# Attention probabilities of 51 units transposed by VectorE blocks and a DRAM exchange instead of by TensorE

## The chip, the cores and the metric

One Trainium2 chip; the kernel runs on one of its cores. The metric is the device time of one launch in microseconds (us), the median of several runs. The engines are named as in the profile: PE (TensorE, with PEld for its weight loads), DVE (VectorE), ACT (ScalarE), POOL (GpSimd) and SP (SyncE, which issues nearly all DMAs here).

## The reference, cut to what matters

A gated cross-attention layer followed by a gated feed-forward layer: B = 8 batches, S = 128 tokens, E = 512, H = 32 heads in 8 key-value groups of 4 heads, D = 128, all float32.

```
q = (layernorm(x) @ Wq) per head, k = ctx @ Wk, v = ctx @ Wv per group; q, k rotated by position
scores = q k^T / sqrt(D); masked scores = -1e9
attn = softmax(scores)                       # 128 queries x 128 keys, per batch and head
x = x + tanh(g_xattn) * (concat(attn @ v) @ Wo)
x = x + tanh(g_ffn) * FFN(layernorm(x))      # silu(x w1 + b1) * (x w2 + b2), then w3, b3
```

What the change touches is `attn @ v`: `attn` stands with queries on the partitions, and the product needs it with keys there, so each 128 x 128 block of probabilities has to be transposed.

## The kernel before

Every float32 product is made of three PE passes over hi and lo parts (`three`, L509 to L511): a value is split into a rounded hi part (ACT) and the remainder lo (DVE or POOL). The kernel has a first stage (transposes of the inputs, K and V projections, the first Q blocks, until about 115 us), then 64 **units**, and a feed-forward stage at the end.

A unit n = 16 gg + 2 c + k (`n_of`) is one key-value group (n // 8) with one batch (n % 8): 4 heads, 128 queries, 128 keys. Its steps, with the engine of each and the line in the profile:

- `scores` (PE, L632 and L633): q k^T of the four heads into `s_banks`, the one PSUM buffer for it; it waits until `mask_rest` of the unit before has read that buffer.
- `mask_first` and `mask_rest` (DVE, L1432 and L1441), then `exps` (ACT, L913, four), `recip` (DVE, L1451) and `norm` (POOL, L1185) make the probabilities in `prob[k]`.
- `prob_transpose` (PE, four transposes, L515) writes them with keys on the partitions to `t_bank`; `pT_hi_copy` (ACT) and `pT_lo_split` (DVE) make the hi and lo parts from there.
- `pv` (PE, three matmuls) into `pv_bank`, then `o_hi_copy` (ACT) and `o_lo_split` (DVE, L1306). The next `pv` waits for both, since there is one `pv_bank`.
- `out_proj` (PE, twelve matmuls) into `o_bank[k]`, and `add_out` (DVE, L1465) to the residual.

Beside each unit stands one Q block of the units to come: `q_block` (PE, twelve matmuls into `f_bank`), `cos_q` and `sin_q` (DVE, L1353), `add_q` (POOL, L1176), later `q_hi_copy` (ACT) and `q_lo_split` (POOL, L1143). One weight chunk a unit is split too (`split_chunk`, ACT and POOL); SP refills its slot of `raw` when POOL is done with it (`load_chunk`, L444).

There is no scheduler: each engine runs its own list in order, with semaphores. After a written-out first pair comes a loop of three passes over eight pairs, then (from unit 52) written-out lists in which the feed-forward weights are prepared too: `ffn_load` (SP, L483, four DMAs a tile), `ffn_tile` (DVE, L1532, a transpose of 32 x 32 blocks), `ffn_hi` (ACT), `ffn_lo` (POOL). In the loop a unit's transpose, `pv` and next unit's scores follow each other on PE like this:

```
q_block, scores(c,1), q_block, prob_transpose(c,0), out_proj(c-1,0), pv(c,0),
prob_transpose(c,1), out_proj(c-1,1), scores(c+1,0), pv(c,1)
```

## Time and profile before

| what | value |
|---|---|
| runs | 665.12 us median of 3 (665.05 to 666.77) |
| span of the profiled execution | 662.9 us (its own time is not listed apart; the median of the runs is 2.2 us above the span) |
| granted TensorE clock | 1.000 |
| PE busy | 654.6 us, 99% |
| DVE, POOL, ACT busy | 490.2 (74%), 385.5 (58%), 314.1 (47%) |
| DMA | 66.32 MB, 100 GB/s mean |

The page lists each engine's busy time and the costliest groups of instructions. A timeline row gives start, length, engine, line, operation, what is written from what, and in square brackets the idle time ahead of it with what ended it. Matmuls are pipelined, so their rows overlap: the distance of two starts tells what one costs, not its length.

### The profile page before, as it was taken

To read this page: it belongs to the slowest core of one execution; us is meant where nothing else is said; L and a number is where in the kernel's file an instruction comes from. 1 tells how busy PE (TensorE), PEld (TensorE's weight loads), DVE (VectorE), ACT (ScalarE), POOL (GpSimd) and SP (SyncE) were. 2 spreads that over 40 slices of the span, in tenths; PEclk is the share of its full clock that TensorE was granted. 3 is DMA by queue.
4 is the path that set the end of the run, shared out by engine and by line. 5 is a ranking of instruction groups with operands and counts; after the bars stand their busy time and mean duration, and the time that the engine had idled before them with its cause. 6 is when DMAs were issued, how large, how long until landed. Compare 5 with 4: busy or idle time off the path is not lost.

```text
span 662.9 us, 11265 instructions
## 1 busy us (share of the span) xinstructions
PE 654.6 (99%) x3309; PEld 550.3 (83%) x3309; DVE 490.2 (74%) x1235; ACT 314.1 (47%) x891; POOL 385.5 (58%) x323
## 2 busy tenths in 40 slices
PE   8999999999999999999999999999999999989998
PEld 7888888788888888888888888888888888878886
DVE  3987665887777777777777777777777888986432
ACT  4335613545445445544554554554455566545210
POOL 6457767875566666666556666666655776402100
PEclk9999999999999999999999999999999999999999
DMA  9996983422212131312222121212122205000002
GB/s 302 321 325 210 306 303 105 143 62 99 91 39 97 44 99 34 95 32 96 62 80 95 34 98 45 95 32 95 63 76 75 58 10 151 0 1 1 0 33 95
DMA packets 67452, 66.32 MB, mean 100 GB/s; under 512 B 6608, under 2 KB 50640, under 8 KB 67408
## 3 DMA queue, kind: packets, MB, share of 16 engines
q1 hardware_dynamic: 65984, 64.77, 30.7%
q0 software_dynamic: 384, 1.05, 0.4%
q8 instruction: 17, 0.28, 0.2%
q14 instruction: 27, 0.22, 0.1%
q10 hardware_dynamic: 1040, 0.00, 0.1%
HBM read 46.93 MB, written 18.87 MB: 99 GB/s over the span
## 4 chain that ended last, share of the span: by engine, by line
PE 94%; DVE 2%; DMA 1%; issue 1%; POOL 0%; ACT 0%; DVEq 0%
PE f_bank L509 12%; PE f_bank L511 12%; PE f_bank L510 12%; PE o_bank L509 10%; PE o_bank L511 10%; PE o_bank L510 10%; PE s_banks L632 6%; PE t_bank L515 4%; PE pv_bank L509 3%; PE pv_bank L511 3%; PE pv_bank L510 3%; PE s_banks L633 2%; PE t_bank L511 1%; PE t_bank L509 1%; PE s_banks L511 1%; PE s_banks L510 1%
## 5 line engine op out<-in xcount | busy, mean ns | idle before, releaser
L1185 POOL TENSOR_TENSOR prob<-prob,small 128x512 f32<-128x512 f32 x64 | 66.6, 1040 | 124.9 <-DVE small L1451 124.9
L913 ACT ACTIVATE prob<-prob,small 128x128 f32<-128x128 f32 x256 | 99.8, 391 | 77.7 <-DVE small L1441 72.2
L509 PE MATMUL o_bank<-wo_hi,o_hi 128*128 128x512 f32 x248 | 102.1, 412 | 0.0
L1143 POOL TENSOR_TENSOR q_lo<-q,q_hi 128x512 fp32r<-128x512 f32 x64 | 82.7, 1292 | 32.8 <-ACT q_hi L843 32.8
L509 PE MATMUL f_bank<-xT_hi,wq_hi 128*128 128x512 f32 x256 | 101.6, 397 | 0.0
L843 ACT ACTIVATE o_hi<-pv_bank 128x512 fp32r<-128x512 f32 x64 | 38.3, 599 | 131.4 <-PE pv_bank L511 130.9
L511 PE MATMUL f_bank<-xT_hi,wq_lo 128*128 128x512 f32 x256 | 99.9, 390 | 0.0
L510 PE MATMUL f_bank<-xT_lo,wq_hi 128*128 128x512 f32 x256 | 99.8, 390 | 0.0
L511 PE MATMUL o_bank<-wo_hi,o_lo 128*128 128x512 f32 x248 | 97.4, 393 | 0.0
L510 PE MATMUL o_bank<-wo_lo,o_hi 128*128 128x512 f32 x248 | 96.9, 391 | 0.0
L1353 DVE TENSOR_TENSOR t_sin<-f_bank,rope 64x512 f32<-64x512 f32 x128 | 88.1, 689 | 2.8
L1176 POOL TENSOR_TENSOR q<-t_cos,t_sin 128x512 f32<-128x512 f32 x64 | 82.7, 1293 | 4.3 <-DVE t_sin L1353 4.2
L1441 DVE CUSTOM_DVE_ANT_0 prob<-s_banks,prob 128x128 f32<-128x128 f32 x256 | 59.1, 287 | 10.3 <-DVE prob L1432 7.7
L1353 DVE TENSOR_TENSOR t_cos<-f_bank,rope 128x512 f32<-128x512 f32 x64 | 43.9, 686 | 29.5 <-PE f_bank L511 29.4
L632 PE MATMUL s_banks<-k_parts,q_hi 128*128 128x256 f32 x256 | 62.8, 323 | 0.4 <-issue 0.2
L1465 DVE SCALAR_TENSOR_TENSOR resid<-o_bank,small,resid 128x512 f32<-128x512 f32 x62 | 46.4, 748 | 17.4 <-PE o_bank L511 16.2
L633 PE MATMUL s_banks<-k_parts,q_lo 128*128 128x128 f32 x256 | 56.9, 222 | 0.0
L511 PEld LDWEIGHTS f_bank<-xT_hi,wq_lo 128*128 128x128 f32 x256 | 48.1, 188 | 10.2
L509 PEld LDWEIGHTS f_bank<-xT_hi,wq_hi 128*128 128x128 f32 x256 | 48.1, 188 | 9.5 <-issue 0.4
L510 PEld LDWEIGHTS f_bank<-xT_lo,wq_hi 128*128 128x128 f32 x256 | 48.2, 188 | 9.1
L511 PEld LDWEIGHTS o_bank<-wo_hi,o_lo 128*128 128x128 f32 x248 | 46.6, 188 | 10.6
L1306 DVE TENSOR_TENSOR o_lo<-pv_bank,o_hi 128x512 fp32r<-128x512 f32 x64 | 44.0, 687 | 15.3 <-ACT o_hi L843 15.3
(170 smaller groups left out, 1469.5 us busy)
## 6 DMA issues: line engine op xcount, KB each, us to landing
k_scratch<-ks_parts SPq DMA_DIRECT2D x16, 512.0 KB, 3.1
raw<-in_L_xattn_Wq_dram SPq DMA_DIRECT2D x32, 256.0 KB, 2.8
raw<-in_L_xattn_Wo_dram SPq DMA_DIRECT2D x32, 256.0 KB, 2.6
k_parts<-k_scratch SPq DMA_DIRECT2D x16, 512.0 KB, 3.6
v_scratch<-vs_hi SPq DMA_DIRECT2D x16, 256.0 KB, 3.9
v_scratch<-vs_lo SPq DMA_DIRECT2D x16, 256.0 KB, 4.3
v_hi<-v_scratch SPq DMA_DIRECT2D x16, 256.0 KB, 3.9
v_lo<-v_scratch SPq DMA_DIRECT2D x16, 256.0 KB, 4.3
```

The source lines that it names most:

```text
L509: nc.tensor.matmul(dst, st[0], mv_[0], start=start, stop=False)
L510: nc.tensor.matmul(dst, st[0], mv_[1], start=False, stop=False)
L511: return nc.tensor.matmul(dst, st[1], mv_[0], start=False, stop=stop)
L632: nc.tensor.matmul(s_banks[:, 256 * h:256 * (h + 1)], q_hi[:, k, h, :], k_parts[:, half, b, :], start=True, stop=False)
L633: mm = nc.tensor.matmul(s_banks[:, 256 * h:256 * h + 128], q_lo[:, k, h, :], k_parts[:, half, b, 0:128], start=False, stop=True)
L913: e = nc.scalar.activation(prob[:, k, h, :], prob[:, k, h, :], ACT.Exp, bias=nmin[k][:, h:h + 1], scale=-1.0, accum_out=psum_row[k][:, h:h ...
L1143: nc.gpsimd.tensor_tensor(dst, a, b_, ALU.subtract).then_inc(s, 1)
L1176: nc.gpsimd.tensor_tensor(q32[:, (e // 4) % 2, e % 4, :], t_cos[:, ts, :], t_sin[:, ts, :], ALU.add).then_inc(pool_rope, 1)
L1185: nc.gpsimd.tensor_tensor(prob[:, k], prob[:, k], rrow[k].unsqueeze(2).to_broadcast([128, GH, S]), ALU.mult).then_inc(pool_norm, 1)
L1353: return nc.vector.tensor_tensor(dst, a, b_, ALU.mult)
L1441: op = nc.vector.tensor_tensor_reduce(prob[:, k, h, :], s_parts[:, h, 0, :], prob[:, k, h, :], 1.0, HUGE, ALU.add, ALU.min, nmin[k][:, h:h ...
L1465: nc.vector.scalar_tensor_tensor(out=resid[:, b, :], in0=bank_of_out(gg, c, k)[:, :], scalar=tg_x, in1=resid[:, b, :], op0=ALU.mult, op1=A ...
```

## The change

For units 2 to 52 PE does no transpose. `p_blocks` on DVE transposes `prob` in 32 x 32 blocks into a new tile `p_blk`, SP stores that tile to a scratch in DRAM (`store_p`, 256 KB) and loads it back with rows and blocks exchanged (`load_p`, 256 KB in runs of 512 bytes) into `p32`. ACT makes `pT_hi` from `p32` and POOL, instead of DVE, makes `pT_lo`. Units 0, 1 and 53 to 63 keep `prob_transpose`. Since the exchange takes time, the loop is written anew: a step of unit u does the scores of u+1, the Q block, `out_proj` of u-2 and `pv` of u-1. The loop covers units 4 to 51, with written-out code ahead of it and behind it. SP's list is fully written out, with the stores and loads between the weight loads. `b3_row` gets its own place, as `p_blk` takes the old one. The diff, cut to its core:

```diff
+HEAD_T, TAIL_T = 2, 11
+        def unit(c, k, d):
+            return (2 * c + k + d) // 2, (2 * c + k + d) % 2
+        def on_pe(n):
+            return isinstance(n, int) and (n < HEAD_T or n >= 4 * UNITS - TAIL_T)
...
 # SP
+            def store_p(gg, c, k):
+                sp.wait_ge(dve_pblk, n + 1 - HEAD_T)
+                sp.dma_start(p_dram[slot * 128:(slot + 1) * 128, :], p_blk[:, k, :]).then_inc(p_stored[k], 16)
+            def load_p(gg, c, k):
+                sp.wait_ge(p_stored[k], 16 * swap_turn(gg, c))
+                if not (isinstance(n, int) and n < HEAD_T + 2):
+                    sp.wait_ge(act_pThi, n - 1)
+                    sp.wait_ge(pool_pTlo, n - 1 - HEAD_T)
+                sp.dma_start(p32[:, k, :].rearrange("p (i x) -> p i x", i=4),
+                             p_dram[slot * 128:(slot + 1) * 128, :].rearrange("(i c) (j x) -> (c j) i x", i=4, j=4)).then_inc(p_loaded[k], 16)
+            def pair(gg, c):
+                store_p(gg, c, 0); load_chunk(2 * r + 1, G + 2); load_p(gg, c, 0)
+                if r == 0 and not first: next_v(1, G)
+                store_p(gg, c, 1); load_chunk(...); load_p(gg, c, 1)
+                # then next_k(0, G + 1) at r == 1, next_v(0, G + 1) at r == 2, next_k(1, G + 1) at r == 3
...
 # PE
+            def step(gg, c, k):
+                scores(gg, *unit(c, k, 1))
+                q_block(gg, 6 + 2 * c + k)
+                out_proj(gg, *unit(c, k, -2))
+                pv(gg, *unit(c, k, -1))
...
 # ACT
             def pT_hi_copy(gg, c, k):
-                act.wait_ge(pe_pT, n + 1)
+                if on_pe(n):
+                    act.wait_ge(pe_pT, turn_of(n))
+                else:
+                    act.wait_ge(p_loaded[k], 16 * swap_turn(gg, c))
...
+                    hi(heads_by_q_block(pT_hi[:, k]), by_q_block(p32[:, k]), act_pThi)
+            def step(gg, c, k):
+                o_hi_copy(gg, *unit(c, k, -2))
+                split_chunk(*pair_chunks(gg, c)[k])
+                q_hi_copy(gg, *unit(c, k, 2))
+                exps(gg, *unit(c, k, 1))
+                pT_hi_copy(gg, c, k)
...
 # POOL
+            def pT_lo_split(gg, c, k):
+                pool.wait_ge(act_pThi, n_of(gg, c, k) + 1)
+                pool.wait_ge(pe_pv, n_of(gg, c, k) - 1)
+                nc.gpsimd.tensor_tensor(heads_by_q_block(pT_lo[:, k]), by_q_block(p32[:, k]), heads_by_q_block(f32(pT_hi[:, k])),
+                                        ALU.subtract).then_inc(pool_pTlo, 1)
+            def step(gg, c, k):
+                split_chunk(*pair_chunks(gg, c)[k])
+                q_lo_split(gg, *unit(c, k, 2))
+                norm(gg, *unit(c, k, 1))
+                add_q(gg, 6 + 2 * c + k)
+                pT_lo_split(gg, c, k)
...
 # DVE
+            def p_blocks(gg, c, k):
+                dve.wait_ge(pool_norm, n + 1)
...
+                nc.vector.transpose(p_blk[:, k, :].rearrange("p (j h b) -> p j h b", j=4, h=GH),
+                                    prob[:, k].rearrange("p h (a j) -> p j h a", j=4)).then_inc(dve_pblk, 1)
+            def step(gg, c, k):
+                mask_scores(gg, *unit(c, k, 1))
+                o_lo_split(gg, *unit(c, k, -2))
+                cos_q(gg, 6 + 2 * c + k)
+                recip(gg, *unit(c, k, 1))
+                sin_q(6 + 2 * c + k)
+                p_blocks(gg, *unit(c, k, 1))
+                add_out(gg, *unit(c, k, -2))
...
 # written-out tail: DVE, ACT and POOL ahead of exps(3, 2, 1) and norm(3, 2, 1), unit 53
             ffn_tile(0)
+            o_lo_split(3, 1, 0)
             o_lo_split(3, 1, 1)
...
             exps(3, 2, 1)
             pT_hi_copy(3, 2, 0)
...
             q_lo_split(3, 3, 0)
-            norm(3, 2, 0)
+            pT_lo_split(3, 2, 0)
             split_chunk(*pair_chunks(3, 2)[0])
             norm(3, 2, 1)
```

Three places show how the order moves. First PE ahead of the loop, in the written-out start. Before, behind the scores of unit 2 (`s_banks`, L632) comes the pv of unit 1, and the loop follows at once:

```order
L633 MATMUL s_banks<-k_parts_64,q_lo_63 128x128
L509 MATMUL pv_bank<-pT_hi_71,v_hi_65 128x512 [waits act_ohi,dve_olo,dve_pTlo,act_pThi]
L510 MATMUL pv_bank<-pT_lo_72,v_hi_65 128x512
L511 MATMUL pv_bank<-pT_hi_71,v_lo_66 128x512
L708 UNCONDITIONAL_BRANCH
```

With the change the scores of unit 3 (the row that waits for `dve_mask`) stand directly behind those of unit 2:

```order
L727 MATMUL s_banks<-k_parts_64,q_lo_63 128x128
L726 MATMUL s_banks<-k_parts_64,q_hi_62 128x256 [waits dve_mask,pool_qlo,act_qhi]
L727 MATMUL s_banks<-k_parts_64,q_lo_63 128x128
L726 MATMUL s_banks<-k_parts_64,q_hi_62 128x256
L727 MATMUL s_banks<-k_parts_64,q_lo_63 128x128
```

What moved is the Q block and the pv of unit 1: both now come behind the scores of unit 3. Second SP, where the loads of the first feed-forward weights are issued (`raw` from `w12`, L483 before). Before, they stand behind the v loads of group 6:

```order
L402 DMA k_parts_64<-k_scratch 128x1024 [waits pe_score]
L407 DMA v_hi_65<-v_scratch 128x512 [waits pe_pv]
L407 DMA v_lo_66<-v_scratch 128x512
L483 DMA raw_58<-in_L0_ffn_w12_dram 32x4x128 [waits pool_wlo,act_whi]
L483 DMA raw_58<-in_L0_ffn_w12_dram 32x4x128 x3
```

With the change the stores and loads of units 50, 51 and 52 and the k load of group 7 stand ahead of them:

```order
L487 DMA p_scratch<-p_blk_101 128x512 [waits dve_pblk]
L497 DMA p32_81<-p_scratch 128x4x128 [waits pool_pTlo,act_pThi,p_stored1]
L431 DMA k_parts_64<-k_scratch 128x1024 [waits pe_score]
L487 DMA p_scratch<-p_blk_101 128x512 [waits dve_pblk]
L497 DMA p32_81<-p_scratch 128x4x128 [waits pool_pTlo,act_pThi,p_stored0]
L568 DMA raw_58<-in_L0_ffn_w12_dram 32x4x128 [waits pool_wlo,act_whi]
L568 DMA raw_58<-in_L0_ffn_w12_dram 32x4x128 x3
```

The first feed-forward load has moved behind the exchange of unit 52. Third POOL at the end of the loop, around the norm of unit 53 (the `prob` row). Before:

```order
L1185 TENSOR_TENSOR prob_70<-prob_70,small_77 128x512 [waits dve_recip]
L1143 TENSOR_TENSOR wo1_lo_87<-raw_58,wo1_hi_86 128x512 [waits act_whi]
L1185 TENSOR_TENSOR prob_70<-prob_70,small_77 128x512 [waits dve_recip]
L1176 TENSOR_TENSOR q32_61<-t_cos_68,t_sin_69 128x512 [waits pool_qlo,act_qhi,dve_rot]
L1143 TENSOR_TENSOR q_lo_63<-q32_61,q_hi_62 128x512 [waits act_qhi]
```

With the change:

```order
L1250 TENSOR_TENSOR q_lo_63<-q32_61,q_hi_62 128x512 [waits act_qhi]
L1298 TENSOR_TENSOR pT_lo_72<-p32_81,pT_hi_71 128x4x4x32 [waits pe_pv,act_pThi]
L1250 TENSOR_TENSOR wo1_lo_89<-raw_58,wo1_hi_88 128x512 [waits act_whi]
L1292 TENSOR_TENSOR prob_70<-prob_70,small_77 128x512 [waits dve_recip]
L1283 TENSOR_TENSOR q32_61<-t_cos_68,t_sin_69 128x512 [waits pool_qlo,act_qhi,dve_rot]
```

In place of the norm of unit 52, which now is done in the loop, stands the lo split of that unit, and it waits for ACT's hi part.

## Rows read from the trace of the kernel before

**Rows 1.** The page's busy line, and the core's span and granted clock.
```profile
PE 654.6 (99%) x3309; PEld 550.3 (83%) x3309; DVE 490.2 (74%) x1235; ACT 314.1 (47%) x891; POOL 385.5 (58%) x323
...
core 0: 662.9 us, clock 1.000
```

**Rows 2.** Timeline of PE, 300 to 316 us: start us, length us, engine, line, operation.
```profile
301.36 0.28 PE L632 MATMUL s_banks<-k_parts,q_hi 128*128 128x256 f32 x1
...
302.23 0.45 PE L509 MATMUL f_bank<-xT_hi,wq_hi 128*128 128x512 f32 x1
...
305.02 0.60 PE L515 MATMUL t_bank<-ident,prob 128*128 128x128 f32 x4
305.37 0.48 PE L509 MATMUL o_bank<-wo_hi,o_hi 128*128 128x512 f32 x1
305.69 0.39 PE L510 MATMUL o_bank<-wo_lo,o_hi 128*128 128x512 f32 x1
...
312.10 0.28 PE L632 MATMUL s_banks<-k_parts,q_hi 128*128 128x256 f32 x1
...
316.44 0.28 PE L632 MATMUL s_banks<-k_parts,q_hi 128*128 128x256 f32 x1
```

**Rows 3.** Timeline of DVE, 300 to 316 us.
```profile
305.97 0.18 DVE L1451 RECIPROCAL small<-small 128x4 f32<-128x4 f32 x1 [0.30 <-ACT prob L913]
...
311.05 1.39 DVE L1353 TENSOR_TENSOR t_sin<-f_bank,rope 64x512 f32<-64x512 f32 x2
312.47 0.75 DVE L1465 SCALAR_TENSOR_TENSOR resid<-o_bank,small,resid 128x512 f32<-128x512 f32 x1
313.17 0.69 DVE L1432 TENSOR_TENSOR prob<-s_banks,mfill 128x512 f32<-128x512 f32 x1
...
314.91 0.69 DVE L1306 TENSOR_TENSOR o_lo<-pv_bank,o_hi 128x512 fp32r<-128x512 f32 x1
```

**Rows 4.** Timeline of POOL, same stretch: a norm and an add_q.
```profile
306.22 1.04 POOL L1185 TENSOR_TENSOR prob<-prob,small 128x512 f32<-128x512 f32 x1 [0.66 <-DVE small L1451]
307.22 1.29 POOL L1176 TENSOR_TENSOR q<-t_cos,t_sin 128x512 f32<-128x512 f32 x1
```

**Rows 5.** Timeline of PE's weight loads, the four of the transposes.
```profile
304.79 0.58 PEld L515 LDWEIGHTS t_bank<-ident,prob 128*128 128x128 f32 x4
```

**Rows 6.** Timeline of ACT, same stretch: the first exp of two units.
```profile
304.28 0.40 ACT L913 ACTIVATE prob<-prob,small 128x128 f32<-128x128 f32 x1 [2.16 <-DVE small L1441]
...
315.03 0.40 ACT L913 ACTIVATE prob<-prob,small 128x128 f32<-128x128 f32 x1 [0.51 <-DVE small L1441]
```

**Rows 7.** Timelines of SP and DVE: feed-forward loads, the first feed-forward transpose.
```profile
481.12 15.38 SPq L483 DMA_DIRECT2D raw<-in_L_ffn_w_dram  x12
...
549.12 7.51 SPq L483 DMA_DIRECT2D ffn_raw<-in_L_ffn_w_dram  x16
...
511.38 0.71 DVE L1532 STREAM_TRANSPOSE w_all<-raw 128x512 f32<-128x512 f32 x1
```

**Rows 8.** DMA issues: out<-in, count, KB each, median us to landing.
```profile
raw<-in_L_xattn_Wq_dram SPq DMA_DIRECT2D x32, 256.0 KB, 2.8
...
out_dram<-resid SPq DMA_DIRECT2D x8, 256.0 KB, 2.0
```

**Rows 9.** Timeline of PE around the start of the loop.
```profile
129.47 0.36 PE L632 MATMUL s_banks<-k_parts,q_hi 128*128 128x256 f32 x1
...
131.18 0.47 PE L509 MATMUL pv_bank<-pT_hi,v_hi 128*128 128x512 f32 x1 [0.59 <-issue]
...
134.98 0.39 PE L632 MATMUL s_banks<-k_parts,q_hi 128*128 128x256 f32 x1 [0.15 <-DVE small L1441]
```

**Rows 10.** Timeline of PE's weight loads in the first microseconds.
```profile
1.54 1.57 PEld L591 LDWEIGHTS pv_bank<-ident 128*128 128x128 f32 x8 [1.54 <-POOL ident L1134]
...
5.95 0.50 PEld L515 LDWEIGHTS s_banks<-ident,ctx_raw 128*128 128x128 f32 x4 [0.44 <-DMA ctx_raw<-in_ctx_dram]
```

**Rows 11.** Four 256 KB loads issued in a row at 126.6 us (line L444).
```profile
DMA to landing us min/median/max: 2.6/3.5/4.3
```

More of the change, by code:

```diff
@@ new lines, in next_k, with next_v @@
+            def next_k(half, G):
+                sp.wait_ge(pe_score, 8 * (G - 1) + 4 * half + 4)
+                load_k(half, G)
+            def next_v(half, G):
+                sp.wait_ge(pe_pv, 8 * (G - 1) + 4 * half + 4)
+                load_v(half, G)
+            def pair(gg, c):
+                G, r = 2 * gg + c // 4, c % 4
+                last = isinstance(gg, int) and G + 2 >= KVH
+                swaps = not (isinstance(gg, int) and on_pe(n_of(gg, c, 0)))
+                if swaps:
+                    store_p(gg, c, 0)
+                if not last:
+                    load_chunk(2 * r + 1, G + 2)
+                if swaps:
+                    load_p(gg, c, 0)
+                if r == 0 and not (isinstance(gg, int) and G == 0):
+                    next_v(1, G)
+                if swaps:
+                    store_p(gg, c, 1)
+                if r < 3 and not last:
+                    load_chunk(2 * r + 2, G + 2)
+                elif r == 3 and not (isinstance(gg, int) and G + 3 >= KVH):
+                    load_chunk(0, G + 3)
+                if swaps:
+                    load_p(gg, c, 1)
+                if r == 1:
+                    next_k(0, G + 1)
+                if r == 2:
+                    next_v(0, G + 1)
+                if r == 3:
+                    next_k(1, G + 1)
@@ L1039, in _ @@
             split_chunk(*pair_chunks(3, 2)[0])
+            o_hi_copy(3, 1, 1)
             exps(3, 2, 1)
@@ L1518, in _ @@
             dve.wait_ge(act_small, 1)
-            first_pair()
+            mask_scores(0, 0, 0)
+            rot_cos(len(ROT_ORDER) - 1, (len(ROT_ORDER) - 1) % 2, 1, False, True)
+            rot_sin((len(ROT_ORDER) - 1) % 2, 1, False)
+            recip(0, 0, 0)
+            cos_q(0, 5)
+            mask_scores(0, 0, 1)
+            pT_lo_split(0, 0, 0)
+            sin_q(5)
+            recip(0, 0, 1)
+            cos_q(0, 6)
+            o_lo_split(0, 0, 0)
+            sin_q(6)
+            pT_lo_split(0, 0, 1)
+            cos_q(0, 7)
+            sin_q(7)
+            mask_scores(0, 1, 0)
+            recip(0, 1, 0)
+            mask_scores(0, 1, 1)
+            p_blocks(0, 1, 0)
+            cos_q(0, 8)
+            recip(0, 1, 1)
+            sin_q(8)
+            p_blocks(0, 1, 1)
+            o_lo_split(0, 0, 1)
+            add_out(0, 0, 0)
+            mask_scores(0, 2, 0)
+            cos_q(0, 9)
+            recip(0, 2, 0)
+            sin_q(9)
+            p_blocks(0, 2, 0)
+            add_out(0, 0, 1)
             with dve.Fori(0, 3) as gg:
-                for c in range(1, 9):
-                    pair(gg, c)
-            pair(3, 1)
+                for c in range(2, 10):
+                    step(gg, c, 0)
+                    step(gg, c, 1)
             def ffn_tile(t):
```

331 lines of the change are left out of this document (160 added, 171 removed).

## The prediction

> **What bounds the kernel now.** I read the page's busy line first: TensorE (PE) is busy 654.6 of 662.9 us and every other engine is at 74% or below [rows 1]. So only what shortens PE's stream, or stops it, moves the end. Then the timeline of PE in the middle of the kernel. One pair of units runs from the score matmuls at 301.36 to the same ones at 316.44: 15.08 us, 7.54 us a unit, with no idle time noted on any row [rows 2]. In it stand the four transposes at 305.02. Behind them the first projection matmul starts 0.35 later, and the second 0.32 after that; undisturbed 512-column matmuls are 0.227 apart (0.87 for scores, then twelve matmuls in 2.79, 302.23 to 305.02). The transposes therefore cost PE 0.35 + 0.09 = **0.445 us a unit**, not the 0.60 of their row.
>
> The sum is made on the span, 662.9; the median of the runs is 2.2 us above it, and I add these 2.2 again at the end.
>
> **Removed from PE.** 51 units x 0.445 = -22.7 us, all on the path as long as PE stays the bound. The unit period would fall from 7.54 to 7.09.
>
> **The steady step, by engine.** Let the score matmuls of unit u+1 start at 0. PE then does scores (0.87), a Q block (2.79), the projection of u-2, pv of u-1. I follow the others with pitches from the timelines.
> VectorE: scores start to mask start is 1.07 (312.10 [rows 2] to 313.17), mask start to the next operation 1.74 (313.17 to 314.91), o_lo 0.69 [rows 3]. So o_lo(u-2) ends at 3.50; a handoff is 0.07 (recip at 305.97, 0.18 long, norm at 306.22 [rows 3, 4]): 3.57. PE wants the weights for that projection at 304.79 - 301.36 = 3.43 [rows 5]: 0.14 late. A weight load runs 0.23 ahead of its matmul (304.79 to 305.02) and needs some 0.13 of that where loads come densely (four in 0.58), so 0.1 is taken up. I take 0.04 us a step: 48 looped steps, **+1.9 us**, bounds 0 and 0.14 (6.7 us).
> VectorE's own loop is mask to exp start 1.86 (313.17 to 315.03), exp to recip 1.69 (304.28 to 305.97) [rows 3, 6], recip 0.2, two sin 1.42 (311.05 to 312.47), the new block transpose, add 0.70. The transpose isn't in this loop before; the nearest row is the weight transpose of equal shape, 0.71 [rows 7]. Sum 6.58, below 7.09: off the path, with 0.5 to spare. It takes the place of the pT_lo split (0.69), so VectorE's load is unchanged.
> GpSimd gets pT_lo: four operations of 1.29 and one norm of 1.04 a step [rows 4], 6.2 of 7.1 us. Norm starts 0.25 after recip (305.97 to 306.22), add_q waits for sin, then pT_lo, the weight split and q_lo follow; the next norm finds it free about 0.7 early. Cost nothing, if pT_lo, with its runs of 32, stays below some 1.9.
> ScalarE copies pT_hi from SBUF instead of PSUM: no change beyond hundredths.
> The exchange: SP stores p_blk (2.0 us to land, as the output rows of this size [rows 8]), waits for the weight split to refill raw, issues that load (0.4), then issues load_p, 512-byte runs as in the Wq loads (2.8 [rows 8]), with the 256 KB load just ahead of it on the queue. pT_hi wants it about 6.6 us into the step and pv(u) only in the next step: hidden. It has a loop of its own, priced as a rival below. The k and v reloads pass the same queue and delay it by 0.5 to 1 us four times in eight units, inside 4 us of slack before pv. 51 x 0.5 MB more traffic lies beside it.
>
> **The head.** Before, PE fills the wait for mask(2) with pv(1) and Q block 8. Now scores(3) stands directly behind scores(2) and waits for mask(2), since s_banks is one buffer. Scores(2) start at 129.47 and are over at 130.4; scores(3) can start at 134.98 as before [rows 9]. PE stands 4.55 us; it stood 0.59 + 0.15 there before, some 0.95 with the refilling of its pipeline, and pv and the Q block come later: **+3.6 us**. Following the chain to the loop (mask(3), exp, norm(3) behind two weight splits and q_lo on GpSimd), scores(5) start 0.25 late, and mask(5), behind add_out(1), holds the first projection of the loop by about 1.2: **+1.4**, bounds 0 and 3.
>
> **The tail.** Here the written-out lists meet the new lag. Three stalls, all on PE:
> First, pv(51) needs o_lo(50). VectorE has ffn_tile(0) ahead of it. Before, its loads were issued at 481.12, 30 us ahead of its use at 511.38 [rows 7]. Now SP issues them behind store_p(52) and load_p(52). With the step's start at 0: block transpose done 6.95, store issued 7.0, landed 9.1, load_p issued 9.2, four ffn pieces at 0.47 each (7.51 for sixteen) from 9.6, the last at 11.0, landed 13.1 (taken like the 2.0 of the stores); ffn_tile 0.65, o_lo 0.69: 14.55. PE wanted the weights at 6.9 (7.09 less one matmul). **+7.5 us**, bounds 6.5 and 9.
> Second, the TensorE transpose of unit 53. GpSimd now does pT_lo(52) and a weight split ahead of norm(53), and pT_lo(52) waits for pT_hi(52), which ScalarE does after exps(53). From the end of scores(53): mask start 0.2, exp 1.86 later, pT_hi 1.6 on (exp to recip 1.69 less a handoff), the copy itself some 0.6, pT_lo 1.25, split 1.25, norm 1.04, handoffs: 7.9. PE has a Q block and a projection in between, 5.45: **+2.5**.
> Third, pv(53) now follows pv(52) with only scores(54) between; o_hi and o_lo in turn need some 1.7: **+0.9** (an estimate: o_hi taken as long as o_lo).
> After that the lists agree with the former order.
>
> **The clock.** The profile's granted clock is 1.000, the 2.4 GHz level [rows 1]. Still, after the idle launch the first weight loads come 0.197 apart (eight in 1.57) and at 5.95 only 0.103 apart (four in 0.50) [rows 10]: half pace from 1.54 to 5.95. An idle 7.5 us in the tail may bring that back: half of 4.4, **+2.2**, bounds 0 and 4.4 (once more after the head's 4.5 us).
>
> **Sum:** 662.9 - 22.7 + 1.9 + 5.0 + 10.9 + 2.2 = 660.2, with 2.2 outside the span **662.4 us** against 665.12.
>
> **A rule against the change.** The block transpose reads prob 4 floats apart, 16 bytes. The trace has only transposes whose reads run on contiguously, 0.71 [rows 7], so it can't speak on the step. The Trainium skill, page "SBUF — State Buffer", section "Door 1: The DMA port swizzle", notes that SBUF has 16-byte lines and that each access which crosses into a new one pays a penalty, of no stated size; it names four fp32 as how far a step stays free, which is just this step. By it the transpose would be longer than 0.71; no row here shows that, and rival C prices it from rows.
>
> **Rivals.**
> A. The exchange becomes the bound: slower than before. Its loop is pT_hi 0.6, handoff 0.1, pT_lo 1.25, weight split 1.29, SP 0.1, issue of the weight load 0.4, load_p L, 0.05: 3.8 + L. At the 2.8 of a lone load it is 6.6; four loads issued back to back landed after 2.6 to 4.3, median 3.5 [rows 11]. It decides from L = 3.4; with 3.5 the step is 7.3 instead of 7.13, 48 x 0.17 = 8 more than forecast: **670.5**; at 4.3 it is 8.1, 709. For it: a 256 KB load always stands 0.4 us ahead. Against: that adds only 0.2 to 0.4 to 2.8. Chance 0.14.
> B. Of the projection's 0.14 nearly nothing is taken up, 0.12 a step instead of 0.04: 48 x 0.08 = 3.8, **666.2**, bounds 664.5 and 667.2. Chance 0.22.
> C. The 16-byte step of the block transpose. Doubled to 1.42, VectorE's loop is 7.3, again 48 x 0.17 = 8: **670.5**. It decides from 1.3. That sin, o_lo and the weight transpose, with very different layouts, all take 0.69 to 0.71 speaks against it. Chance 0.12.
> D. The stalls are smaller, with no fall of the clock and the start-up absorbed: 662.4 - 2.2 - 1.4 = **658.8**. Chance 0.10.
> E. The forecast, 659.5 to 664. Chance 0.42.
>
> **The numbers.** Runs of this kernel tell apart about 0.3%, 2 us: below 663.1 is faster, above 667.1 slower. Faster: D (0.10) and four fifths of E (0.34): 0.44. Same: the rest of E (0.08) and B (0.22) but for its upper edge (0.01): 0.29. Slower: A (0.14), C (0.12) and that edge: 0.27. The range takes D's lower edge, 657.5, and reaches into A and C, 673.
>
> **What would show it.** PE's period in the loop (7.1 right; 7.3 or more means A or C, told apart by the block transpose's row and by what pT_hi waits for); PE idle ahead of scores(3) of 4.5 us, ahead of pv(51) of 7.5, ahead of the transposes of unit 53 of 2.5; weight loads 0.2 apart after them. It is wrong if the loop's projections wait for o_lo by 0.1 or more, or if ffn_tile(0) finds its data.

## The result

The changed kernel takes 674.44 us (median of 4 runs, 671.20 to 675.56) against 665.12: a ratio of 1.0128, 95% interval 1.0101 to 1.0155. It is slower by 1.3%, where 0.4% faster was forecast, and lies 1.4 us above the range. The profiled execution took 673.71 us, with a span of 671.8, so 1.9 lie outside the span.

The page of the profiled execution, its busy line and, of the 40 equal slices of the span, the granted TensorE clock in tenths (compare [rows 1]); the core's span and its mean granted clock stand in the fence behind it:

```profile
PE 641.7 (96%) x3105; PEld 532.3 (79%) x3105; DVE 517.4 (77%) x1235; ACT 318.5 (47%) x891; POOL 451.3 (67%) x374
...
PEclk9999999979999999899999989999997999999999
```

```profile
core 0: 671.8 us, clock 0.984
```

PE is busy 12.9 us less than before, and yet the span is 8.9 longer: PE now stands still, and where the clock's digit drops below 9 it also runs slower. So the reading goes to where PE stands. First the steady loop, as PE's timeline (start, length, engine, line, operation) shows it between two score matmuls (compare [rows 2]):

```profile
294.26 0.28 PE L726 MATMUL s_banks<-k_parts,q_hi 128*128 128x256 f32 x1
...
297.93 0.40 PE L603 MATMUL o_bank<-wo_hi,o_hi 128*128 128x512 f32 x1
...
301.35 0.28 PE L726 MATMUL s_banks<-k_parts,q_hi 128*128 128x256 f32 x1
```

The step is 7.09 us, as the forecast had it, and PE's matmuls wait for nothing in it. Now all rows of PE's timeline behind 130 us, up to the feed-forward stage, ahead of which PE stood for over 0.3 us (in brackets the idle time and what ended it):

```profile
135.41 0.55 PE L726 MATMUL s_banks<-k_parts,q_hi 128*128 128x256 f32 x1 [4.49 <-DVE small L1559]
...
157.50 0.47 PE L603 MATMUL o_bank<-wo_hi,o_hi 128*128 128x512 f32 x1 [1.04 <-DVE o_lo L1420]
...
274.93 0.70 PE L603 MATMUL o_bank<-wo_hi,o_hi 128*128 128x512 f32 x1 [2.69 <-DVE o_lo L1420]
...
393.67 0.47 PE L603 MATMUL o_bank<-wo_hi,o_hi 128*128 128x512 f32 x1 [2.42 <-DVE o_lo L1420]
...
513.99 0.76 PE L603 MATMUL pv_bank<-pT_hi,v_hi 128*128 128x512 f32 x1 [7.70 <-DVE o_lo L1420]
...
527.82 0.66 PE L609 MATMUL t_bank<-ident,prob 128*128 128x128 f32 x4 [2.16 <-POOL prob L1292]
...
533.42 0.47 PE L603 MATMUL pv_bank<-pT_hi,v_hi 128*128 128x512 f32 x1 [0.63 <-DVE o_lo L1420]
```

Five of the seven were in the forecast. The two at 274.93 and 393.67 were not: they lie where the loop goes into its second and third pass. There VectorE, which PE waits for, stands without any releaser (VectorE's timeline, first pass end):

```profile
267.56 1.11 DVE L1579 STREAM_TRANSPOSE p_blk<-prob 128x512 f32<-128x512 f32 x1
268.70 0.75 DVE L1595 SCALAR_TENSOR_TENSOR resid<-o_bank,small,resid 128x512 f32<-128x512 f32 x1
272.03 0.69 DVE L1550 TENSOR_TENSOR prob<-s_banks,mfill 128x512 f32<-128x512 f32 x1 [2.58 <-issue]
...
273.77 0.69 DVE L1420 TENSOR_TENSOR o_lo<-pv_bank,o_hi 128x512 fp32r<-128x512 f32 x1
```

add_out ends the pass at 269.45; the scores that the next mask reads (from 268.42) are there at 269.4, but mask starts at 272.03, after 2.58 us of "issue", which is time in which an engine waits for nothing that the profile shows. o_lo behind it is late by as much, and so is PE's projection. Last, what PE does behind its stops: the granted clock by windows (from:to, length, then busy us of each engine with its instructions, the granted clock, DMA share and GB/s):

```profile
135.40:141.90 6.50, 6.49 (x19) 5.49 (x20) 2.84 (x11) 4.25 (x18) 4.66 (x4) 0.50 0.29 89
274.90:278.00 3.10, 3.07 (x8) 2.45 (x9) 2.51 (x5) 1.17 (x5) 1.65 (x2) 0.52 0.00 0
514.00:517.40 3.40, 3.40 (x8) 2.72 (x9) 0.69 (x1) 1.04 (x2) 0.00 (x0) 0.51 0.45 108
527.80:531.70 3.90, 3.88 (x19) 3.30 (x20) 0.69 (x1) 1.12 (x2) 3.90 (x4) 1.00 0.23 67
```

And PE's timeline, matmuls behind the stop at 274.93:

```profile
275.43 0.63 PE L604 MATMUL o_bank<-wo_lo,o_hi 128*128 128x512 f32 x1
275.86 0.63 PE L605 MATMUL o_bank<-wo_hi,o_lo 128*128 128x512 f32 x1
...
278.66 0.39 PE L603 MATMUL o_bank<-wo_hi,o_hi 128*128 128x512 f32 x1
278.88 0.40 PE L604 MATMUL o_bank<-wo_lo,o_hi 128*128 128x512 f32 x1
```

Behind the stops of 4.49, 2.69 and 7.70 us the granted clock is 0.50 to 0.52, the 1.2 GHz level, and matmuls come 0.43 apart; from 278.66 they are 0.23 apart again. I call these stretches half pace. Behind the stop of 2.16 the clock stayed at 1.00 in this trace.

The exchange itself, by the page's groups (GpSimd's pT_lo, ScalarE's pT_hi, each with busy us, mean ns and the idle time ahead of it) and by its DMA issues (the load-back, with its median us to landing):

```profile
L1298 POOL TENSOR_TENSOR pT_lo<-p,pT_hi 128x512 fp32r<-128x512 f32 x51 | 66.1, 1295 | 22.1 <-ACT pT_hi L945 21.7
...
L945 ACT ACTIVATE pT_hi<-p 128x512 fp32r<-128x512 f32 x51 | 32.3, 633 | 100.7 <-DMA p<-p_scratch 100.7
...
p<-p_scratch SPq DMA_DIRECT2D x51, 256.0 KB, 3.1
```

ScalarE waits for it in 47 of the 51 units, PE never does in the loop.

**Where the 8.9 us of span come from**, each term from the rows above or from the starts of the scores of each unit:

| term | forecast | measured |
|---|---|---|
| 51 transposes off PE | -22.7 | -22.7 (step of 7.09 instead of 7.54) |
| projection waits for o_lo in each step | +1.9 | 0 in the ordinary step |
| stop ahead of scores(3), against 0.74 before | +3.6 | +3.75 |
| start-up (step to unit 6: 8.38 instead of 7.09) | +1.4 | +1.3 |
| tail: 7.70 + 2.16 + 0.63 | +10.9 | +10.5 |
| half pace: 3.1 behind scores(3), 1.7 + 1.7 at the pass ends, 1.6 in the tail | +2.2 | +8.1 |
| the stops at the two pass ends, 2.69 + 2.42 | none | +5.1 |
| six steps of 7.37 to 7.63 and some of 7.16 to 7.22 in the loop, less 0.63 of the like before | none | +2.1 |
| first stage (scores(0) at 115.06, before 114.73) | none | +0.3 |
| sum | -2.7 | +8.5, of 8.9 |

The half pace is taken from stretches of equal work: scores and Q block behind the first stop took 6.74 (135.41 to 142.15) instead of 3.66, projection and pv behind the two pass ends 5.12 and 5.11 instead of 3.42 (297.93 to 301.35), pv and Q block in the tail 5.10 instead of 3.47.

The six steps of 7.37 to 7.63 are those with the first projection of a new group (units 8, 16, up to 48). In them PE's first weight load of the projection comes 0.31 to 0.40 us behind the end of o_lo, in the other steps 0.07. What it waits for there stays open.

### The profile page after: what moved, and what is told of

Read it like the earlier page. It is cut to its first block, busy times and chain, and to the rows that moved or that the text cites. A ratio compares the mean times of both kernels' runs of the same rounds, so it can differ in the third digit from the quotient of the medians.

```text
span 671.8 us, 10945 instructions
## 1 busy us (share of the span) xinstructions
PE 641.7 (96%) x3105; PEld 532.3 (79%) x3105; DVE 517.4 (77%) x1235; ACT 318.5 (47%) x891; POOL 451.3 (67%) x374
## 4 chain that ended last, share of the span: by engine, by line
PE 69%; POOL 11%; issue 11%; DVE 6%; DMA 1%; ACT 1%; POOLq 0%; DVEq 0%; ACTq 0%
PE f_bank L603 9%; PE f_bank L604 9%; PE f_bank L605 9%; PE o_bank L603 7%; PE o_bank L605 7%; PE o_bank L604 7%; PE s_banks L726 4%; POOL q_lo L1250 3%; POOL pT_lo L1298 3%; PE pv_bank L603 3%; PE pv_bank L605 2%; PE pv_bank L604 2%; POOL q L1283 2%; POOL wq_lo L1250 2%; POOL wo_lo L1250 2%
## 5 line engine op out<-in xcount | busy, mean ns | idle before, releaser
L603 PE MATMUL o_bank<-wo_hi,o_hi 128*128 128x512 f32 x248 | 100.2, 404 | 7.2 <-DVE o_lo L1420 7.0
L603 PE MATMUL f_bank<-xT_hi,wq_hi 128*128 128x512 f32 x256 | 104.6, 408 | 0.0
L604 PE MATMUL f_bank<-xT_lo,wq_hi 128*128 128x512 f32 x256 | 101.2, 395 | 0.0
L1283 POOL TENSOR_TENSOR q<-t_cos,t_sin 128x512 f32<-128x512 f32 x64 | 82.8, 1293 | 22.8 <-DVE t_sin L1467 22.7
L1298 POOL TENSOR_TENSOR pT_lo<-p,pT_hi 128x512 fp32r<-128x512 f32 x51 | 66.1, 1295 | 22.1 <-ACT pT_hi L945 21.7
L945 ACT ACTIVATE pT_hi<-p 128x512 fp32r<-128x512 f32 x51 | 32.3, 633 | 100.7 <-DMA p<-p_scratch 100.7
L603 PEld LDWEIGHTS o_bank<-wo_hi,o_hi 128*128 128x128 f32 x248 | 47.1, 190 | 25.7 <-issue 15.7
L1579 DVE STREAM_TRANSPOSE p_blk<-prob 128x512 f32<-128x512 f32 x51 | 56.6, 1110 | 1.5
```

The lines of the kernel that those rows point to most:

```text
L603: nc.tensor.matmul(dst, st[0], mv_[0], start=start, stop=False)
L604: nc.tensor.matmul(dst, st[0], mv_[1], start=False, stop=False)
L1283: nc.gpsimd.tensor_tensor(q32[:, (e // 4) % 2, e % 4, :], t_cos[:, ts, :], t_sin[:, ts, :], ALU.add).then_inc(pool_rope, 1)
L1298: nc.gpsimd.tensor_tensor(heads_by_q_block(pT_lo[:, k]), by_q_block(p32[:, k]), heads_by_q_block(f32(pT_hi[:, k])), ALU.subtract).then_inc ...
```

## Experiments

All edits are to the changed kernel unless said otherwise. Starts of scores are numbered by unit, so "step 22" is the time from scores(21) to scores(22), the first step of the loop's second pass that is done late.

### VectorE's loop written out

```diff
 # DVE
-            with dve.Fori(0, 3) as gg:
+            for gg in range(3):
                 for c in range(2, 10):
                     step(gg, c, 0)
                     step(gg, c, 1)
```

> VectorE's loop over three passes is written out, its order kept; nothing else differs from the changed kernel (674.4 us, span 671.8). Theory (the stall sits at VectorE's jump back): the 2.58 and 2.36 us ahead of mask of units 21 and 37 go, with them PE's 2.69 and 2.42 us ahead of the projections at 274.93 and 393.67 and the half pace behind each; the two long steps, 11.63 and 11.36, become 7.1: -8.8 us, 665.6. Rival (the stall is the exchange's, or that of another engine's loop): the two steps stay at 11.4 to 11.6, 674. Rival (any code of this length is fetched late): the two stalls turn into others of a like size at other places, 670 to 674.

Measured: 665.79 us (10 runs), ratio to the kernel before 1.0012 (1.0002 to 1.0022). Steps 22 and 38 are 7.45 and 7.44 instead of 11.63 and 11.36. VectorE at the place of the first pass end:

```profile
267.69 0.75 DVE L1595 SCALAR_TENSOR_TENSOR resid<-o_bank,small,resid 128x512 f32<-128x512 f32 x1
268.50 0.69 DVE L1550 TENSOR_TENSOR prob<-s_banks,mfill 128x512 f32<-128x512 f32 x1
```

mask follows add_out at once. So the jump back of VectorE's loop was the cause of both stops and of the half pace behind them, and neither the exchange nor another engine's jump was: the other engines kept their loops. The two steps together are 8.1 us shorter; the medians differ by 8.65, but other steps and the tail differ between the two traces as well. The remaining 0.35 of steps 22 and 38 has another cause, and no run here separates it.

### The tail in another order

```diff
 # SP
-            for p in range(2, 26): pair(p // 8, p % 8)
-            store_p(3, 2, 0); load_p(3, 2, 0); ffn_load(0); ffn_load(1); ffn_load(2)
+            for p in range(2, 25): pair(p // 8, p % 8)      # the last pair is written out behind it
+            store_p(3, 1, 0); ffn_load(0); load_p(3, 1, 0)
+            store_p(3, 1, 1); ffn_load(1); load_p(3, 1, 1); next_k(0, KVH - 1)
+            store_p(3, 2, 0); ffn_load(2); load_p(3, 2, 0)
 # PE
-            pv(3, 1, 1); q_block(3, 10)
+            q_block(3, 10); pv(3, 1, 1)
...
-            pv(3, 2, 1); q_block(3, 12)
+            q_block(3, 12); pv(3, 2, 1)
 # DVE
-            ffn_tile(0); o_lo_split(3, 1, 0); o_lo_split(3, 1, 1); cos_q(3, 10)
+            o_lo_split(3, 1, 0); ffn_tile(0); cos_q(3, 10); o_lo_split(3, 1, 1)
 # ACT
-            exps(3, 2, 1); pT_hi_copy(3, 2, 0)
+            pT_hi_copy(3, 2, 0); exps(3, 2, 1)
 # POOL
-            split_chunk(*pair_chunks(3, 2)[0]); norm(3, 2, 1)
+            norm(3, 2, 1); split_chunk(*pair_chunks(3, 2)[0])
```

> The tail alone is put in another order: SP issues the first three feed-forward loads between a store and its load-back (units 50, 51, 52), PE does a Q block ahead of pv(51) and ahead of pv(53), VectorE does o_lo(50) ahead of the first feed-forward tile, ScalarE pT_hi(52) ahead of exps(53), GpSimd norm(53) ahead of a weight split. Theory (the three tail stalls were these orders): PE's 7.70, 2.16 and 0.63 us go, and 1.4 us of half pace behind the first: -11.9, 662.5. Rival (the feed-forward loads then delay the load-back of units 50 to 52, so pv waits for it): 2 to 4 us of it come back, 665 to 667.

Measured: 657.62 us, ratio 0.9884 (0.9867 to 0.9900). The changed kernel, first SP's timeline, then VectorE's:

```profile
508.42 0.37 SPq L497 DMA_DIRECT2D p<-p_scratch  x1
508.88 5.68 SPq L568 DMA_DIRECT2D raw<-in_L_ffn_w_dram  x12
```

```profile
512.55 0.71 DVE L1661 STREAM_TRANSPOSE w_all<-raw 128x512 f32<-128x512 f32 x1 [5.39 <-DMA raw<-in_L_ffn_w_dram]
513.19 0.65 DVE L1420 TENSOR_TENSOR o_lo<-pv_bank,o_hi 128x512 fp32r<-128x512 f32 x1
```

This kernel, SP's timeline and then VectorE's:

```profile
490.67 1.82 SPq L568 DMA_DIRECT2D raw<-in_L_ffn_w_dram  x4
```

```profile
505.64 0.68 DVE L1425 TENSOR_TENSOR o_lo<-pv_bank,o_hi 128x512 fp32r<-128x512 f32 x1
506.23 0.70 DVE L1666 STREAM_TRANSPOSE w_all<-raw 128x512 f32<-128x512 f32 x1
```

In the changed kernel the first feed-forward load is issued at 508.88, behind load_p(52), and VectorE holds o_lo(50) back for it until 513.19. Here the loads start at 490.67, and o_lo goes first. From scores(52) to scores(55) it takes 25.40 us (497.59 to 522.99) instead of 37.90: 12.5 off, as the theory's 11.9 had it. The median fell by more, 16.8. Part of that is which executions were profiled: the old tail is short in the trace of the changed kernel. The same stretch takes 39.5 to 40.5 in the seven other traces that keep the old tail without added matmuls (40.38 with VectorE's loop written out), and the profiled execution of this kernel was its longest, 659.97 us. In the kernel with VectorE's loop written out PE ran slow behind the second stop as well (its window behind that stop, columns as above):

```profile
519.00:522.00 3.00, 2.96 (x11) 2.49 (x12) 0.69 (x1) 1.11 (x2) 3.00 (x3) 0.67 0.35 87
```

The same stop of 2.2 us was followed by a granted clock of 0.67 there and of 1.00 in the profile of the changed kernel. This is probably part of why the changed kernel's runs scatter from 671.2 to 675.6; only one of them has a trace. The five orders were changed together, so the run shows what they are worth as a whole and not one by one.

### The start in another order

```diff
 # PE
             scores(0, 1, 0)
-            scores(0, 1, 1); q_block(0, 8); out_proj(0, 0, 0); pv(0, 0, 1); scores(0, 2, 0); q_block(0, 9)
+            q_block(0, 8); pv(0, 0, 1); scores(0, 1, 1); out_proj(0, 0, 0); q_block(0, 9); scores(0, 2, 0)
             out_proj(0, 0, 1)
 # DVE: mask(2) ahead of pT_lo(1); recip(2) ahead of sin 7; p_blocks(2) ahead of mask(3); o_lo(1) ahead of recip(3); mask(4) ahead of add_out(0)
 # ACT: o_hi(1) ahead of q_hi(4);  POOL: norm(2) ahead of add_q(7)
```

> The written-out start alone is put in another order: PE does Q block 8 and pv(1) between scores(2) and scores(3), VectorE does mask(2) as soon as scores(2) are there and o_lo(1) ahead of the block transpose of unit 3. Theory (VectorE is then the bound of the start): PE's 4.49 us ahead of scores(3) and the 3.0 us of half pace behind it go, but VectorE's own work from mask(2) to mask(5) is 18.4 us, so mask(5) starts 4.6 earlier: -4.6, 669.8. Rival (the start is bound by PE alone): -7.5, 666.9. Rival (the wait comes back whole in the first steps of the loop): 674.

Measured: 671.69 us, ratio 1.0117 (1.0076 to 1.0159), 2.75 below the changed kernel, less than either number and within the scatter of the runs. scores(4) start at 141.26 instead of 145.58, but two steps on most of these 4.32 us are gone: scores(6) start at 159.78 instead of 161.02, 1.24 earlier. PE's timeline shows where, and ScalarE's what stood ahead of pv(2):

```profile
147.08 0.47 PE L603 MATMUL pv_bank<-pT_hi,v_hi 128*128 128x512 f32 x1 [1.88 <-issue]
...
149.68 0.58 PE L726 MATMUL s_banks<-k_parts,q_hi 128*128 128x256 f32 x1 [1.67 <-POOL q_lo L1250]
```

```profile
145.00 0.63 ACT L945 ACTIVATE pT_hi<-p 128x512 fp32r<-128x512 f32 x1 [4.28 <-DMA p<-p_scratch]
```

The stop has moved: pv(2) now waits for the exchange of unit 2 (ScalarE's copy waits for its load-back until 145.00, GpSimd's pT_lo ends at 146.97), and scores(5) for what stands behind that on GpSimd. The theory held VectorE for the next in line and did not look at SP, whose store of unit 2 is queued behind three weight loads.

### The three edits together

> The three edits of the runs above together. Theory (three places, each with its own stall, nothing else lost): -8.8 - 11.9 - 4.6 = -25.3, 649 us, 0.976 of the kernel before. Rival (something else sets the end once these are gone): 655 or more.

Measured: 650.95 us, ratio 0.9787 (0.9770 to 0.9803). The loop and the tail have no stop left over 0.3 us; the 1.95 us above the 649 of the sum fit the start, where the two waits of the run before are still there (1.97 and 1.68): scores(6) start 2.5 us earlier than in the changed kernel, and the theory had 4.6.

### Block transposes that read on contiguously

```diff
-                                    prob[:, k].rearrange("p h (a j) -> p j h a", j=4)).then_inc(dve_pblk, 1)
+                                    prob[:, k].rearrange("p h (j a) -> p j h a", j=4)).then_inc(dve_pblk, 1)
```

> The block transpose reads runs of 32 floats instead of every fourth float, nothing else differs from the changed kernel; keys then land in another order, so the products of the exchanged units are not the reference's. Theory (the 16-byte step is the transpose's extra price): its row falls from 1.11 to 0.71, as the weight transposes, and PE's step in the loop stays 7.10, since VectorE's loop is below it either way; the stalls stay, 671 to 675 us. Rival (the extra price is the permuted destination or the size): the row stays at 1.11. Rival (VectorE is already the bound of the loop): the step falls by up to 0.4, 655.

Measured: 672.12 us in one run. The block transposes by their tile (shortest/median/longest of 51 in ns), in the changed kernel:

```profile
L1579 DVE STREAM_TRANSPOSE p_blk<-prob x51: 1092/1110/1125, 139.1 to 505.3; 128x512 f32<-128x512 f32 x51
```

And in this one:

```profile
L1579 DVE STREAM_TRANSPOSE p_blk<-prob x51: 706/712/715, 138.8 to 501.2; 128x512 f32<-128x512 f32 x51
```

The step of 16 bytes costs 0.40 us an operation: the rule of the Trainium skill, page "SBUF — State Buffer", section "Door 1: The DMA port swizzle", that an access which crosses into a new 16-byte line pays a penalty, is borne out here in kind. That four fp32 is a step which stays free, as it also says, is not: these reads are just that far apart and took 1.11 us instead of 0.71. In the loop the price is hidden all the same: PE's step stays at 7.08 to 7.11, since VectorE's loop, at 6.58 + 0.40, is still below it. Rival C's mechanism exists, at 1.11 us, under the 1.3 from which it would have decided.

### Matmuls in place of idle time

```diff
+            def keep_busy(count):
+                for i in range(count):
+                    nc.tensor.matmul(o_bank[0][:, :], xT_hi[:, 0, 0:128], xT_hi[:, 1, 0:512], start=True, stop=True)
...
             scores(0, 1, 0)
+            keep_busy(18)
             scores(0, 1, 1)
...
+            pe.wait_ge(dve_acc, n_of(3, 1, 0) + 1)
+            keep_busy(31)
             pv(3, 1, 1)
```

> The changed kernel with 18 matmuls of 512 columns, whose result nothing reads, ahead of scores(3), and 31 ahead of pv(51): PE works through most of the 4.49 and 7.70 us in which it stood. Theory (the half pace is the price of standing idle): scores(3) and pv(51) start when they did, but at 0.227 a matmul, so 3.0 us behind the first place and 1.4 or more behind the second come back: 669 to 670. Rival (half pace has another cause, a change in what PE computes or the memory traffic): no change, 674. Rival (the added matmuls are in the way): slower than 674.

Measured: 668.07 us (5 runs), ratio 1.0062 (1.0034 to 1.0089), 6.4 below the changed kernel although PE does 49 matmuls more. scores(3) start at 135.23, as before (135.41), and pv(51) 14.96 us behind scores(52), as before (14.95). What is different is the clock behind them (windows of this kernel, columns as above):

```profile
135.20:141.90 6.70, 6.67 (x33) 5.70 (x34) 4.73 (x15) 4.27 (x18) 4.84 (x5) 1.00 0.33 103
508.30:511.80 3.50, 3.44 (x15) 2.88 (x16) 0.69 (x1) 1.12 (x2) 0.00 (x0) 1.00 0.60 184
```

1.00 where it was 0.50 and 0.51. So the half pace comes from the standing itself. Of the 3.0 us of the first place most is lost again in the next steps (scores(6) start 1.6 earlier, scores(11) 0.6), and the step behind pv(51) is 1.6 shorter: 2.2 us of the 5.6 by which the spans of the two traces differ. The rest lies where nothing was edited: the two pass ends cost 1.9 and 2.1 us in this trace instead of 4.5 and 4.3, with no slow stretch behind them, and the step to scores(54) is 1.6 longer, with one. So the runs do not show that all of the 6.4 is due to the added matmuls. Behind stops of 1.7 to 2.7 us the half pace comes in some traces and not in others: the stop of 2.69 us at the first pass end was followed by a granted clock of 0.52 in the changed kernel, one of 2.69 in the kernel shifted by 296 waits (below) by 1.00, one of 1.82 in the kernel shifted by 320 by 0.63.

### VectorE's loop shifted by idle waits

```diff
 # DVE, ahead of the blocks of the first stage (80 and 160: directly behind pos_fix)
+            for _ in range(N):
+                dve.wait_ge(pos_loaded, 16)
```

> 80 more wait instructions, all on a semaphore long since reached, stand near the start of VectorE's list, so that its loop lies 80 instructions further on; nothing else differs from the changed kernel. Theory (the jump back costs 2.5 us because of where the loop's code lies against what the engine holds): the stalls of 2.58 and 2.36 us ahead of mask of units 21 and 37 can vanish or stay with the place, and at one of the two shifts (80, 160) they differ from those of the changed kernel by over 1 us. Rival (every jump back of this loop costs the same, and before it was hidden): 2.4 to 2.6 at both shifts.

> The same with 160 wait instructions. Theory (where the code lies decides): at one of the two shifts the stalls differ by over 1 us. Rival (each jump back costs the same): 2.4 to 2.6 at both. The waits take some 8 us at a place where VectorE has nothing to do; the time is not what is looked at.

> 16 wait instructions on a semaphore long since reached stand in VectorE's list where it is idle (after 11 us), so that its loop starts at instruction 275 of its list instead of 259; nothing else differs from the changed kernel. So far: start 259 stalls at the jump back, 339 doesn't, 419 does. Theory (the loop of 358 instructions stalls when it reaches into three blocks of 256, with a count that begins 4 to 8 before mine): 275 to 632 lies in two blocks, so no stall, steps 22 and 38 at 7.5, -8.3 us, 666. The Trainium skill, page 'Runtime: NRT & Kernel Launch', section 'Instruction fetch mechanics', gives the engine a memory of two blocks of 256 instructions and says that a jump to what is not in it waits for a fetch; by it alone, without the measured start numbers, one could not tell at which shift. Rival (the place decides in another way, by some period near 160): 275 lies beside 259, stalls of 1.6 to 2.6 us stay, 673.

> 148 such waits: the loop lies at 407 to 764, 12 instructions short of the place that stalled (419 to 776). Theory (three blocks of 256 or two): 764 is still in the second block, no stall, steps 22 and 38 at 7.5. Rival (a gradual effect of the place): a stall near the 1.7 and 2.6 us of 419. The waits cost some 9 us in the first stage; the time is not what is looked at.

These expectations count a wait instruction that holds two waits as one. The 80 of them took 8.10 us (first row below), 0.05 us for each of 160 waits, so I count waits one by one from here: the shifts are 160, 320, 32 and 296. The kernels shifted by 160, 320 and 296 have one run each, 680.59, 691.23 and 680.77 us; their first stage ends later by the waits (scores(0) at 125.76, 130.49 and 123.78 instead of 115.06), so the time is not what they are for. VectorE's timeline at a shift of 160, with add_out and mask at the first jump back:

```profile
12.76 0.69 DVE L1422 TENSOR_TENSOR cT_lo<-s_banks,cT_hi 128x512 fp32r<-128x512 f32 x1 [8.10 <-issue]
...
280.36 0.75 DVE L1597 SCALAR_TENSOR_TENSOR resid<-o_bank,small,resid 128x512 f32<-128x512 f32 x1
281.14 0.69 DVE L1552 TENSOR_TENSOR prob<-s_banks,mfill 128x512 f32<-128x512 f32 x1
```

At a shift of 320, the mask behind each jump:

```profile
286.06 0.69 DVE L1552 TENSOR_TENSOR prob<-s_banks,mfill 128x512 f32<-128x512 f32 x1 [1.72 <-issue]
...
405.07 0.69 DVE L1552 TENSOR_TENSOR prob<-s_banks,mfill 128x512 f32<-128x512 f32 x1 [2.59 <-issue]
```

At a shift of 32, and then of 296, the mask behind the first jump:

```profile
271.13 0.69 DVE L1552 TENSOR_TENSOR prob<-s_banks,mfill 128x512 f32<-128x512 f32 x1 [2.99 <-issue]
```

```profile
280.55 0.69 DVE L1552 TENSOR_TENSOR prob<-s_banks,mfill 128x512 f32<-128x512 f32 x1 [2.58 <-issue]
```

At a shift of 160 mask follows add_out directly; steps 22 and 38 are 7.55 and 7.54. At the three others it stands 1.6 to 3.0 us, and the kernel shifted by 32 takes 672.39 us (1.0101, interval 1.0083 to 1.0119). So where the same code lies decides, and nothing in the work does. My first rule, that a loop stalls when it touches three blocks of 256 instructions, fell at 32 and at 296. Counted wait by wait from the first instruction of my list, the opposite fits:

| VectorE's loop | instructions | blocks of 256 touched, if one begins at 0 | idle at the jumps, us |
|---|---|---|---|
| changed kernel | 261 to 618 | 2 | 2.58, 2.36 |
| shifted by 32 | 293 to 650 | 2 | 2.99, 2.19 |
| shifted by 296 | 557 to 914 | 2 | 2.58, 1.56 |
| shifted by 320 | 581 to 938 | 2 | 1.72, 2.59 |
| shifted by 160 | 421 to 778 | 3 | none |
| kernel before | 219 to 560 | 3 | none |

### The kernel before, with its loop shifted

The last run puts that rule to the test on another kernel: 64 waits more in the kernel before, at a place where VectorE is idle.

> The kernel before, with 64 waits on a semaphore long since reached in VectorE's list where it is idle, so that its loop (342 instructions, waits counted one by one) lies at 283 to 624 instead of 219 to 560. So far, counted the same way: loops that touch two blocks of 256 stalled at the jump back (261 to 618, 293 to 650, 557 to 914, 581 to 938), loops that touch three did not (421 to 778, and 219 to 560 in this kernel). Theory (two blocks stall, three do not): VectorE now stands 1.5 to 3 us without a releaser at the two jumps, behind mask of units 20 and 36 and ahead of o_lo; in this order o_lo and cos_q have some 1 us to spare there, so 0.5 to 2 us reach PE at each: 666 to 669. Rival (the six fit by chance, or only the new loop is concerned): no idle time at the jumps, 665.0.

Measured: 666.54 us (9 runs), ratio 1.0020 (1.0010 to 1.0030). VectorE behind the two jumps, where the kernel before has no idle time:

```profile
257.06 0.69 DVE L1306 TENSOR_TENSOR o_lo<-pv_bank,o_hi 128x512 fp32r<-128x512 f32 x1 [2.64 <-issue]
...
378.95 0.69 DVE L1306 TENSOR_TENSOR o_lo<-pv_bank,o_hi 128x512 fp32r<-128x512 f32 x1 [2.92 <-issue]
```

The rule forecast this one rightly: 2.64 and 2.92 us. But so does its mirror image. If the engine's blocks begin 70 to 106 instructions further on than I count them, the five loops that stall touch three blocks and the two that do not touch two, for all seven. Where a block begins no run shows.

The traces speak for the mirror image, since they hold the loads of code as a DMA kind of its own ("instruction"). From 262 to 520 us, two passes with both jumps, the queue of these loads in the changed kernel and then in the one shifted by 160 (packets, MB, share):

```profile
q14 instruction: 11, 0.09, 0.1%
```

```profile
q14 instruction: 1, 0.01, 0.0%
```

The loop that does not stall is hardly loaded again at all; those shifted by 32, 296 and 320 take 11, 11 and 12 loads in the same window. With the loop written out there are 7 and no stop, so a load alone does not make a stop. In each of the 18 stops of VectorE at a jump, in nine kernels, one such load starts within 0.6 us of the stop's start (269.99 in the changed kernel, where the stop is 269.45 to 272.03). So the stop comes together with code being loaded again, and where the loop is not loaded again there is no stop. The trace does not say for which engine a load is.

The old order of work hides nearly all of the stop: the steps concerned are 11.67 and 11.95 instead of 11.04 and 11.09, 0.6 and 0.9 us, against 4.5 and 4.3 in the changed kernel. There PE, behind the jump, wants o_lo first and stands 2.4 to 2.7 us, then runs at half pace; here it stands 0.71 and 0.98 us and keeps its pace.

### The three edits and an earlier exchange at the start

```diff
 # SP, on top of the three edits
-            pair(0, 0); pair(0, 1)      # load_chunk 1, 2, store_p(2), load_chunk 3, load_p(2), store_p(3), load_chunk 4, load_p(3)
+            load_chunk(1, 2); store_p(0, 1, 0); load_p(0, 1, 0); load_chunk(2, 2); load_chunk(3, 2)
+            store_p(0, 1, 1); load_p(0, 1, 1); load_chunk(4, 2); next_k(0, 1)
```

> The three edits together (650.95 us) and SP's first stores and load-backs ahead of the weight loads that wait for GpSimd: store and load-back of unit 2 behind one load instead of three, load-back of unit 3 ahead of one load. Theory (pv(2) waits 1.97 us for the exchange there, scores(5) 1.68 for what stands behind it on GpSimd; then VectorE's list is next): 2 of these 3.6 us come back, 649. Rival (VectorE's list is the bound already): 651, no change.

Measured: 648.13 us (647.86 to 648.98), ratio 0.9746 (0.9730 to 0.9762): 2.5% faster than the kernel before and 3.9% faster than the change as it came. Its profiled execution has a span of 647.1 us at a granted clock of 1.000. pv(2) no longer waits; scores(5) still wait 1.69 us for GpSimd and the loop's first projection 1.72 for o_lo, so the start is the next place to look.

## Why the prediction was wrong, point by point

- **The gain, -22.7: right.** PE's step fell from 7.54 to 7.09 and no engine's loop became the bound. Rival A did not come: the load-back landed after 3.1 us (median of 51), below the 3.4 from which it decides. GpSimd's pT_lo took 1.295 us, below the 1.9 allowed.
- **Projection behind o_lo, +1.9 (rival B +5.7): the lateness right, its price wrong.** In the ordinary step o_lo ends 3.50 us behind the scores' start, as forecast, and the weight load comes 0.07 later. But the matmul starts 0.10 behind its weight load instead of 0.23, so all of the lateness is taken up (the step from 294.26):

```profile
297.83 0.19 PEld L603 LDWEIGHTS o_bank<-wo_hi,o_hi 128*128 128x128 f32 x1 [0.17 <-issue]
```

- **Block transpose at 0.71: wrong, 1.11,** without cost, as 0.5 us were to spare. The trace of before could not speak on the 16-byte step; the run with contiguous reads did.
- **Head, start-up and tail: right.** 4.49 for 4.55, 1.3 for 1.4, 7.70 for 7.5 (the forecast's own terms, 14.55 less 6.9, give 7.65), 2.16 for 2.5, 0.63 for 0.9. Each was found by following the written-out lists by hand, and the run with the tail reordered confirmed the causes in the tail, taken together.
- **The clock, +2.2: mis-sized, 8.1.** I allowed for one slow stretch behind one stop, with "once more" as a bound. There were four, of 1.6 to 3.1 us each, one behind each of the four longest stops. It should have been added to each long stop that I forecast: 3.1 + 1.6 make 4.7 before any surprise.
- **The step that failed: the loop taken as 48 equal steps.** "48 looped steps" holds three passes with two jumps back between them, and the sum had no term for a jump. It cost 5.1 us of standing and 3.4 of half pace, 8.5 in all; the run with the loop written out is 8.65 faster, which is the difference between slower by 1.3% and no change by my bound (665.79). With 8.5 for the jumps and 4.7 instead of 2.2 for the clock, the same sum gives 662.4 + 8.5 + 2.5 = 673.4, against 674.44 measured. That it comes so near is in part luck: the 1.9 for o_lo, which did not come, stands in it for the 2.1 of the long steps, which it did not have.
- **Could it be read from the trace of before?** In part. ScalarE stood there twice without a releaser, at exactly the pass ends, and PE's steps there were 11.04 and 11.09 instead of 10.75 (ScalarE's timeline of the kernel before):

```profile
256.49 0.40 ACT L913 ACTIVATE prob<-prob,small 128x128 f32<-128x128 f32 x1 [2.61 <-issue]
...
377.53 0.40 ACT L913 ACTIVATE prob<-prob,small 128x128 f32<-128x128 f32 x1 [2.66 <-issue]
```

I passed over them since they cost PE 0.3 us. They suggest that a jump back can cost an engine 2.6 us, and that the old order had slack for it. The loads of code were to be seen there too: five in one pass (253.9 to 374.9), and ten in the same window of the shifted kernel, in which VectorE stands as well. Whether VectorE would pay it could not be read there; a term of 0 to 2 x 4.5 us belonged in the range, and the new step, in which mask and o_lo stand first behind the jump and PE waits for o_lo with 0.1 to spare, was the worst place for it.
